# Adaptive attention and GRU on one core: score products in 64x32 tiles over two PSUM banks, V copied once and laid out by DMA, VectorE's order changed

## What is computed

```python
def _L0(x, emb, ...):                    # attention, 16 heads of 16
    scale, shift = jnp.split(emb @ W_emb + b_emb, 2, axis=-1)
    xn = _rms_norm(x, g_norm) * (1.0 + scale) + shift
    q, k, v = ...(xn @ W_qkv)
    q = _rms_norm(q, g_q); k = _rms_norm(k, g_k)
    attn = softmax(einsum('bhqd,bhkd->bhqk', q, k) * d ** (-0.5))
    o = einsum('bhqk,bhkd->bhqd', attn, v)
    return o + o @ W_out
x = x + _L0(x, cond[:, None, :], ...)
x = x + GRU(initial_state=cond, inputs=x, ...)   # 32 steps, one after another
```

## Time and profile before

| | |
|---|---|
| time, median of 3 runs | 385.61 us (385.48 to 385.67) |
| span of the profiled execution | 383.5 us |
| busy: PE, DVE, ACT, POOL | 92%, 68%, 70%, 55% |
| attention stage | to about 214 us |
| mean granted TensorE clock | 0.985 |
| chain that ended last | PE 81%, issue 5%, POOL 4%, ACT 4% |

### The profile page before, as it was taken

How to read it: one execution, slowest core, us unless ns; L and a number is a source line. 1 busy time by engine, 2 the same in 40 slices (tenths; PEclk the granted TensorE clock), 3 DMA queues, 4 the chain that set the end, 5 groups by cost and what they waited for, 6 DMA issues and landing times.

```text
span 383.5 us, 11231 instructions
## 1 busy us (share of the span) xinstructions
PE 354.0 (92%) x3795; PEld 305.9 (80%) x3795; DVE 260.9 (68%) x693; ACT 268.9 (70%) x760; POOL 210.3 (55%) x383
## 2 busy tenths in 40 slices
PE   4287999999999999999997899999999999999983
PEld 3165678778777877877775899999999999999982
DVE  3455888888898888889888355555555555555553
ACT  2468999999999999999873555555555555555552
POOL 5347777776777777677742244444444444434432
PEclk9679999999999999999999999999999999999999
DMA  8942211211221121122121000000000000000000
GB/s 264 361 156 57 58 43 43 57 44 43 53 55 38 44 55 43 40 55 50 45 55 24 1 2 29 27 29 27 27 27 27 27 27 27 27 27 27 28 30 27
DMA packets 14269, 20.39 MB, mean 53 GB/s; under 512 B 2578, under 2 KB 7076, under 8 KB 14244
## 3 DMA queue, kind: packets, MB, share of 16 engines
q1 hardware_dynamic: 13700, 18.76, 17.3%
q10 hardware_dynamic: 544, 1.31, 0.9%
HBM read 7.48 MB, written 4.19 MB: 30 GB/s over the span
## 4 chain that ended last, share of the span: by engine, by line
PE 81%; issue 5%; POOL 4%; ACT 4%; DVE 2%; DMA 2%; POOLq 0%; SPq 0%; DVEq 0%; ACTq 0%
PE bank L914 39%; PE bank L961 21%; PE bank L1095 7%; PE bank L1054 4%; PE bank L1108 4%; PE bank L1123 2%; DMA x_in<-in_x_dram 2%; PE bank L1004 2%; PE bank L1019 2%; POOL oT_lo L425 1%; POOL operands L401 1%; POOL xn L415 1%; PE bank L974 1%; ACT square_x L516 1%; ACT v_diag L600 0%
## 5 line engine op out<-in xcount | busy, mean ns | idle before, releaser
L961 PE MATMUL bank<-h,w_hh_sb 128*128 128x128 f32 x768 | 96.9, 275 | 1.4 <-DVE h L902 1.4
L961 PEld LDWEIGHTS bank<-h,w_hh_sb 128*128 128x128 f32 x768 | 91.1, 192 | 2.0 <-DVE h L902 1.8
L676 ACT ACTIVATE operands<-bank,bsum 128x128 f32<-128x128 f32 x64 | 23.6, 368 | 55.6 <-PE bank L961 52.7
L887 DVE SCALAR_TENSOR_TENSOR operands<-bank,vec_cols,operands 128x128 f32<-128x128 f32 x64 | 22.3, 349 | 52.5 <-ACT operands L676 52.5
L486 POOL TENSOR_TENSOR operands<-operands,h 128x128 f32<-128x128 f32 x64 | 29.5, 461 | 51.3 <-ACT operands L677 51.3
L914 PE MATMUL bank<-pair_hi,wih_hi 128*128 128x256 f32 x180 | 52.6, 292 | 0.0
L914 PE MATMUL bank<-pair_hi,wih_lo 128*128 128x256 f32 x180 | 50.2, 279 | 0.0
L914 PE MATMUL bank<-wqkv_hi,xn_hi 128*128 128x512 f32 (+1 forms) x128 | 47.5, 371 | 2.9 <-POOL xn_lo L435 2.9
L914 PE MATMUL bank<-pair_lo,wih_hi 128*128 128x256 f32 x180 | 50.2, 279 | 0.0
L600 ACT COPY v_diag<-bank 32x256 f32<-32x256 f32 x128 | 46.6, 364 | 2.2 <-PE bank L914 0.7
L493 POOL TENSOR_TENSOR operands<-h,x2T 128x256 f32<-128x256 f32 x32 | 23.2, 726 | 41.1 <-issue 30.3
(11 more groups left out here) (107 smaller groups left out, 868.5 us busy)
## 6 DMA issues: line engine op xcount, KB each, us to landing
operands<-operands SPq DMA_DIRECT2D x128, 64.0 KB, 2.0
x_in<-in_x_dram SPq DMA_DIRECT2D x8, 512.0 KB, 8.7
out_dram<-operands SPq DMA_DIRECT2D x16, 256.0 KB, 2.0
stage_w<-in_L_cond_W_qkv_dram ACTq DMA_DIRECT2D x1, 768.0 KB, 7.3
w_hh_sb<-in_L_cond_W_hh_dram SPq DMA_DIRECT2D x1, 768.0 KB, 9.5
stage_w<-in_L_cond_W_ih_dram SPq DMA_DIRECT2D x1, 768.0 KB, 7.4
w_emb_sb<-in_L_cond_W_emb_dram ACTq DMA_DIRECT2D x1, 512.0 KB, 4.6
stage_wo<-in_L_cond_W_out_dram SPq DMA_DIRECT2D x1, 256.0 KB, 6.1
```

Source lines behind the costliest of these rows:

```text
L676: act.activation(r_g[:, c, :], r_in, ACT.Sigmoid, bias=bsum[:, c:c + 1]).then_inc(r_ready[c], 1)
L887: dve.scalar_tensor_tensor(out=rh[:, c, :], in0=xnh[:, HN_COL:HN_COL + B], scalar=bhh[:, 2 * KC + c:2 * KC + c + 1], in1=r_g[:, c, :], op0 ...
L961: last = pe.matmul(dst, gate(w_hh_sb, name, c)[k], moving, start=k == 0 and (name == "n" or opens and name == "z"), stop=k == KC - 1, skip ...
```

## The change

- Scores: each score product is cut in two halves of 64 rows, in 64x32 tiles; half i writes to its own PSUM bank (p_s is now two banks). 32 matmuls of 128 columns replace 16 of 256, and k_diag shrinks to two blocks. The order of the heads in the score columns changes, and the PV products index it accordingly.
- PSUM: to free a bank, p_xT and p_w (output projection) share one. Hence new waits on PE: the transposes of xhat wait for x2_ready, the output projection for xmod_ready.
- V: one ACT copy of 128x256 into v_rows replaces four copies of 32x256; SP then issues four more DMAs per body that lay v_rows out in v_diag. The PV products wait for these.
- PE's order: transposes of q and k now come ahead of the scores, which stand right before the PV products.
- DVE's order: residual, qkn, recip, o_sb, Tp, oT, xmod, ss, ms4, maxima, logits. Exp now works in place on logits. ACT's and POOL's lists keep their order.

```diff
+        s_tiles = [p_s[:, BANK * i:BANK * i + D] for i in range(2)]
...
-        gru_banks = ((p_qkT, p_xT, p_qk[0], p_qk[1]), (p_vx2, p_s, p_o, p_w))
+        gru_banks = ((p_qkT, p_qk[0], p_qk[1], p_s[:, 0:BANK]), (p_vx2, p_s[:, BANK:2 * BANK], p_o, p_xTw))
...
+                v = group(base, u, LAG_V)
+                if v is not None:
+                    slot = (u - LAG_V) % 2
+                    if isinstance(v, int) and v == 0:
+                        sp.wait_ge(ones_ready, 2)
+                    sp.wait_ge(v_ready, v + 1)
+                    for b in range(GB):
+                        rows = slice(T * b, T * b + T)
+                        sp.dma_start(v_diag[rows, (u - LAG_V) % 4, b, :, :].rearrange("p h f -> p (h f)"),
+                                     v_rows[rows, slot, :, :].rearrange("p h f -> p (h f)"))\
+                          .then_inc(v_diag_ready[slot], 16)
...
-                    values(range(0, 2))
+                    act.copy(v_rows[:, (u - LAG_V) % 2, :, 0:DH],
+                             p_v.rearrange("p (h d) -> p h d", h=HEADS)).then_inc(v_ready, 1)
...
-                if v is not None:
-                    values(range(2, GB)).then_inc(v_ready, 1)
...
             def body(base, u):
+
+                if not draining(base, u):
+                    residual(group(base, u, LAG_OUT + 1), (u - LAG_OUT - 1) % 2)
+                g = group(base, u, LAG_QKT)
+                if g is not None:
+                    slot = (u - LAG_QKT) % 2
+                    dve.wait_ge(rs_ready, g + LAG_QK + 1)
+                    if later(g, 2):
+                        dve.wait_ge(qkT_ps, g - 1)
+                    dve.tensor_tensor(qkn[:, slot, :].rearrange("p (h d) -> p h d", d=DH),
...
                 o = group(base, u, LAG_OUT)
...
-                if not draining(base, u):
-                    residual(group(base, u, LAG_OUT + 1), (u - LAG_OUT - 1) % 2)
...
-                g = group(base, u, LAG_QKT)
-                if g is not None:
-                    slot = (u - LAG_QKT) % 2
-                    dve.wait_ge(rs_ready, g + LAG_QK + 1)
...
+                    d = group(base, u, LAG_X2T)
+                    if d is not None:
+                        pe.wait_ge(x2_ready, d + 1)
                     for c in range(KC):
                         last = pe.transpose(p_xT[:, c * P:c * P + P], xhat[:, (u - LAG_MOD) % 2, c * P:c * P + P],
...
+                    m = group(base, u, LAG_MOD)
+                    if m is not None:
+                        pe.wait_ge(xmod_ready, m + 1)
...
-                    pe.wait_ge(v_ready, g + 1)
+                    pe.wait_ge(v_diag_ready[(u - LAG_PV) % 2], spread(g, (u - LAG_PV) % 2))
...
+                if scores is not None:
+                    slot = (u - LAG_S) % 2
+                    for c in range(KC):
+                        for b in range(GB):
+                            for i in range(2):
+                                rows = slice(2 * PB * i, 2 * PB * i + 2 * PB)
+                                last = pe.matmul(s_tiles[i][T * b:T * b + T, c * P:c * P + P]
+                                                 .rearrange("p (r n k) -> p n r k", r=2, k=T),
+                                                 qkT[rows, slot, c * P + T * b:c * P + T * b + T],
+                                                 k_diag[rows, slot, :, :, GB * c + b, :], start=True, stop=True)
+                    last.then_inc(s_ps, 1)
```

More of the change, by code:

```diff
@@ L212, in adaptive_attention_gru @@
         v_ready = sem("v_ready")
+        v_diag_ready = [sem("v_diag_ready0"), sem("v_diag_ready1")]
         qkT_ps = sem("qkT_ps")
@@ L453, in _ @@
             pool.memset(threes[:, :], 3.0).then_inc(threes_ready, 1)
[L454 to L458, removed]
+            pool.memset(v_rows[:, :, :, DH:VW], 1.0).then_inc(ones_ready, 1)
+            pool.memset(v_diag[:, :, :, :, :], 0.0).then_inc(ones_ready, 1)
             pool.wait_ge(threes_ready, 1)
-            pool.wait_ge(ones_ready, 1)
+            pool.wait_ge(ones_ready, 2)
             first = [norm_first[:, i, :] for i in range(7)]
@@ L564, in body @@
                     act.wait_ge(logits_ready, g + 1)
-                    if later(g, 2):
-                        act.wait_ge(probsT_ready, g - 1)
-                    act.activation(probs[:, slot, :], logits[:, slot, :], ACT.Exp).then_inc(probs_ready, 1)
+                    act.activation(logits[:, slot, :], logits[:, slot, :], ACT.Exp).then_inc(probs_ready, 1)
                 if draining(base, u) and draining(base, u - 1):
@@ L595, in body @@
                        .then_inc(oT_hi_ready, 1)
[L597 to L602, removed]
                 v = group(base, u, LAG_V)
@@ L608, in body @@
                         act.wait_ge(o_ps, v - 3)
-                    if isinstance(v, int) and v == 0:
-                        act.wait_ge(ones_ready, 1)
+                    if later(v, 2):
+                        act.wait_ge(v_diag_ready[(u - LAG_V) % 2], spread(v - 2, (u - LAG_V) % 2))
                 d = group(base, u, LAG_X2T)
@@ L1032, in output_projection @@
                         pe.wait_ge(x2_ready, g)
-                    products(p_w[:, 0:D], [oT_hi[:, slot, c * P:c * P + P] for c in range(KC)],
+                    products(p_w, [oT_hi[:, slot, c * P:c * P + P] for c in range(KC)],
                              [oT_lo[:, slot, c * P:c * P + P] for c in range(KC)],
```

68 lines of the change are left out of this document (31 added, 37 removed).

## The result

The kernel after takes 401.25 us (median of 4 runs, 400.5 to 402.31), the kernel before 385.64 (4 runs, 385.48 to 385.79): a ratio of 1.0388, 95% interval 1.0358 to 1.0417. The forecast was 398.2 with a range of 391 to 403, and slower with 0.87. The profiled execution has a span of 398.6 us against 383.5.

A forecast was written before the change was run, and what follows sets the result against it. PE bounds the kernel at 5.61 us a body; the new DVE order closes a 6.09 us ring. Loop +12.0, filling +1.1, draining -0.5 give +12.6 on 383.5: 396.1, plus 2.1 for the median: 398.2 us, range 391 to 403.

The forecast's parts named there:

- rival 3: Attention loop: dependent instruction pairs cost more in the hardware loop; 6.3 us a body, 403 us; chance 0.13.
- The ring: Loop body: qkn through xmod, xn and Newton to the next qkn sets the pitch, 6.09 us against 5.61.
- the filling: Bodies 4 to 8: xmod 0.6 us later in body 4 and another 0.6 in body 8; +1.1 us, estimated.
- signs of being wrong: Attention loop: PE without holes near 5.1, qkn not released by rs, 1 us score block, PE waiting for a DMA.
- PE's block: Scores on PE: 1.00 us shrinks by 0.46 for the rounds, with 0.09 for one tile switch saved; about 0.55 long.
- Rival 5: Scores on PE: the row halves don't run side by side; PE's body 5.5 us, time unmoved; chance 0.1, inside the forecast.
- Rival 4: Score matmuls on PE: a fixed issue time binds; PE's body about 6.5 us, time about 408; chance 0.02.
- Rival 2: Loop body: only the ring through the residual counts; 5.57 to 5.65 us a body, 385 to 387 us; chance 0.05.
- the draining: From xmod of body 33 on: -1.35, about -0.3 and +1.1 us, together -0.5 us.
- the DMAs at SP: SP's list: eight DMAs take 4.8 us to issue, below any pitch considered, covered by several us; no cost.
- GRU stage: Stage after attention, with other banks and the same products: 0 us change.
- Rival 1: Attention loop: PE's saving comes through; pitch 5.1 us, -12.8 us, 373 us; chance 0.08.

The follow-up runs named there:

- late_v: Kernel after, with the last group's four V DMAs issued behind the last keys' DMAs at SP; 398.49 us, ratio 1.0326 to the kernel before.
- order_only: Kernel before with DVE's new order (residual and qkn at the top of the body) and nothing else; 404.7 us, ratio 1.0456.
- old_orders: Kernel after with DVE's and PE's old orders, except that the scores' waits stand ahead of the V products; 384.21 us, ratio 0.9936.
- half_v_late: half_v with ACT's v_rows copy first, its two direct copies behind exp, and the last V DMAs behind the last keys'; 379.22 us, ratio 0.9801.
- v_copies: old_orders, but V by ACT's four copies as before and no V DMAs; 385.29 us, ratio 0.9972 to the kernel before.
- old_dve_order: Kernel after with DVE's old order and PE's new order kept; 393.15 us, ratio 1.0167 to the kernel before.
- half_v: old_orders, but two of four sequences' V copied by ACT straight into v_diag, two by v_rows and DMA; 386.27 us, ratio 1.0006.

## Why the prediction was right, point by point

The measured time lies in the range. At 401.25 it is just above the 394 to 401 that the forecast gave to its own mechanism and inside the stretch that it gave to rival 3. The ring and its pitch came as forecast. Every other term came out on the slow side, and the missing 3 us are not rival 3's: they are the filling, the last group's DMAs, and how far the median lies above the profiled execution. One of the listed signs of being wrong did appear, at the ends of the stage alone: PE waited for a DMA before scores, 0.2 us once in the filling, then 0.24 and 2.29 for the last two groups.

**PE's block.** The score block was forecast at 0.55 and takes 0.59. The stretch in which the switches lie, from the last V product to the PV products, takes 150.96 - 149.72 = 1.24, against 147.57 - 145.78 = 1.79: 0.55 less, which is the forecast (0.46 for the rounds, 0.09 for a switch). The waits added on PE for the residual and for xmod appear in no view: between 60 and 200 us PE's only wait is that for oT_lo, 21.5 us in 23 bodies. Rival 5, halves not side by side, is out: eight rounds of 0.115 would take 0.92. The Trainium skill (TensorEngine Tiling (Array Packing), Key Properties) says that different tiles can load weights and multiply in parallel; the 0.59 agrees. Rival 4, issue, is out as well: 32 score matmuls in 0.59 are 0.018 each. By the 62 ns per MATMUL that the Trainium skill (TensorE: Matmul & The Clock Gate, Back-to-back issue gap) gives for hardware decoding off, they would take an estimated 2.0 us; this trace doesn't agree with that case. (The clock's digit in the earlier trace rows is 9 from the fourth slice on, not from the sixth; nothing in the prediction hangs on it.)

**The ring.** Step by step, forecast and measured:

| step | forecast | in the body from 150.64 |
|---|---|---|
| xmod, to its end | 0.38 | 0.39 |
| end of xmod to xn | 0.18 | 0.17 |
| xn to the first Newton step | 2.06 | 2.06 |
| Newton, to the end of the last | 1.24 | 1.24 |
| to qkn | 0.03 | 0.03 |
| qkn to recip | 0.60 | 0.61 |
| recip to o_sb | 0.29 | 0.28 |
| o_sb to Tp | 0.35 | 0.34 |
| Tp to oT | 0.63 | 0.63 |
| oT to xmod | 0.33 | 0.32 |
| sum | 6.09 | 6.07 |

Over 25 bodies that is 152.43 - 140.28 = +12.15 against +12.0. That the mean of 6.10 meets the forecast's 6.09 so closely is in part luck. The written-out bodies 8 to 10 take 5.98, the twenty of the hardware loop 6.12. From the end of xmod to xn is 0.08 in the former (52.92 + 0.38 to 53.39) and 0.18 in the latter, and the forecast took 0.18 for all. From the last Newton step to qkn is 0.12 instead of 0.03 in two of four loop bodies; in this one POOL's last step ends at 166.41 + 0.26 = 166.67:
```profile
166.79 0.69 DVE L772 TENSOR_TENSOR qkn<-bank,rs 128x512 f32<-128x512 f32 x1 [0.44 <-POOL rs L466]
```
In every fourth body xn comes 0.28 after xmod, but then Newton follows 1.95 after xn instead of 2.06, so this adds nothing. So rival 3's mechanism exists: the loop costs 0.14 a body over the written-out bodies, of which the forecast had 0.10 in its sum; the rest, and what the written-out bodies save, nearly cancel. The 1.95 is POOL's own work between the two, forecast at 1.93. PE's idle time before the output projection was forecast at 1.0 and is 0.91.

**Rival 2, the residual's ring.** The residual starts at 153.68 and would let qkn start 0.35 later, at 154.03; qkn starts at 154.53, released by rs. So that ring alone would give 6.07 - 0.50 = 5.57, which is the forecast's sum for it, and it is out as the limit.

**The filling: +1.1 forecast, +2.24 measured, but not all of it is the change's.** The xmods of bodies 2, 4, 5, 6, 7 and 8 are later than before by 0.34, 1.58, 2.34, 1.77, 1.62 and 2.24. In late_v, whose instructions are the same up to the draining, bodies 4 to 8 are later by 1.52, 1.80, 0.96, 0.79 and 1.41. The two part in body 5, where xmod waits 0.40 for PE in the kernel after (31.13) and not in late_v. Busy time of the same two us in the kernel after and in late_v (PE, PEld, DVE, ACT, POOL; then the granted clock, 1.00 being 2.4 GHz):
```profile
30.00:32.00 2.00, 2.00 (x10) 1.76 (x8) 1.56 (x3) 0.60 (x1) 1.37 (x3) 0.50 0.00 0
```
```profile
30.00:32.00 2.00, 1.39 (x11) 1.01 (x10) 1.78 (x4) 1.02 (x3) 1.56 (x2) 1.00 0.00 0
```
The granted clock was at its lower level (1.2 GHz) in this execution of the kernel after, and had been 0.73 in the two us before; late_v had 1.00 in both. Before the clock fell, PE had been busy for 2.47 of the 4 us from 22 on and for 0.53 of the next 2; in late_v for 3.44 and 0.47. No run tests what set the two apart. So 0.83 of the 2.24 belongs to the execution. Of the 1.41 that late_v has, 0.27 is loading: over the twelve kernels profiled here the first xmod starts anywhere from 14.50 to 15.05, and at 14.85 in order_only, which changes nothing ahead of it. The jump in body 8, 0.62, is recip and o_sb, as forecast with 0.6.

What remains is body 4, and here the +1.1 had luck. It counted 0.6 for the duration of qkn alone. Timeline of DVE there, in the kernel after:
```profile
25.12 0.69 DVE L772 TENSOR_TENSOR qkn<-bank,rs 128x512 f32<-128x512 f32 x1 [1.86 <-POOL rs L466]
25.73 0.41 DVE L820 TENSOR_TENSOR xmod<-bank,mod_scale 128x256 f32<-128x256 f32 x1
```
In body 4 xmod could start at 24.15 in the kernel before, when rs of that body was not there yet (24.51 + 0.26). Put behind qkn, xmod pays for qkn's wait as well as for its duration: 1.58 - 0.34 = 1.24. In an in-order list a moved instruction brings its wait along. That step was sized at half, but the bodies behind it make up for the other half, which the forecast had not in its sum either: in late_v 0.79 - 0.27 = 0.52 of it is left in body 7.

**The draining.** xmod of body 33 to qkn of body 34 is 203.06 - 199.36 = 3.70 instead of 5.25, so -1.55 for the -1.35 forecast; up to recip of body 36 it is -0.40, for the -0.5 forecast in all. Then comes what the prediction had set to nothing: the DMAs at SP. For the body it was right (SP has 4.9 of 6.1 us to do). It failed for the last group, where the keys' DMAs are what PE waits for and stand behind 2.50 us of V issues: +1.15, and late_v takes 1.39 off, more than all of it. Behind that wait the granted clock falls for some 4 us, which is in the +1.15 too. Busy time in stretches of the kernel after, columns as above:
```profile
217.00:219.70 2.70, 0.45 (x5) 0.26 (x3) 2.33 (x5) 0.83 (x3) 0.95 (x1) 1.00 0.32 74
219.70:222.00 2.30, 2.26 (x67) 1.69 (x67) 1.26 (x2) 0.00 (x0) 0.29 (x1) 0.58 0.00 0
222.00:224.00 2.00, 1.97 (x33) 1.71 (x35) 1.89 (x6) 1.00 (x3) 0.00 (x0) 0.63 0.01 4
```
PE was nearly idle from 217.0 to 219.7; then the clock is at its lower level (1.2 GHz) for most of two stretches (1.00 again from 224 on), and the score block, 0.59 in the loop, lasts 220.57 - 219.74 = 0.83. In the kernel before, where the last scores wait 0.48, and in late_v, where they wait 0.92, the granted clock is 1.00 in these stretches.

**The rest.** GRU stage: 0 forecast; from recip of body 39 to the end it is 174.3 before and 174.2 after. The median lies 2.65 above the span of the profiled execution, where 2.1 was taken from the kernel before; the profiled one was the shortest of the four runs. In sum: +12.0, +1.1, -0.5, 0 and 2.1 gave 398.2; +12.15, +2.24, +0.75, 0 and 2.65 give 401.3.

**What PE's and ACT's savings were worth.** The forecast said: hidden. old_orders shows them laid open in its late bodies (5.23), half_v_late shows them paid out (379.2). Rival 1 put them at 373, with a pitch of 5.1; what it missed is that the next limits, ACT with xn_hi and SP's issue, lie close: the pitches found here run from 5.2 to 5.6. Four of my expectations (old_orders, v_copies, old_dve_order, half_v) missed by 3 to 8 us: each took one limit away, and named the wrong next one, none, or one too small; old_orders and old_dve_order missed at the end of the stage besides.

## What to carry to other kernels

When an instruction moves ahead in an in-order list, look up who makes its input and on what that depends: if the way leads back to something now behind it in the same list, a ring through one loop body has closed, and its sum, not any engine's busy time, is the pitch. If the same work is dear inside the suspected ring and free outside it, the ring is real. The slack of the input (here 1.9 us between rs and qkn) is the first number to read; here the ring showed in the trace as engines that all waited, each for another, in every body. Before moving a wait, look at what now stands behind it. Count the issue time of DMAs as work of the engine that issues them, against the pitch hoped for and not the present one, and look at the last group apart, where no later body covers a late transfer.

## What the hardware showed

- Issuing a DMA from one part of SBUF to another costs SP 0.60 to 0.62 us here, with 64 KB (keys) and with 34 KB (V) alike: four in 2.41 to 2.50.
- In old_orders and the kernel after, up to about 90 us and again near the end of the stage, one of four such issues often takes 0.6 to 1.3 us longer (3.16, 3.62 and 3.25 us above). What else the chip does at that time I didn't find; the cause stays open.
- In the filling, one 128x33 step on POOL takes 0.66 us instead of 0.26, in both kernels, while DVE makes wo_lo from two tiles in SBUF. In the kernel after, newton_b (L462) starts at 28.67 and lasts 0.66, DVE's wo_lo (L746) starts at 28.53 and lasts 0.69: POOL's step ends 0.11 after DVE's. The Trainium skill (SBUF — State Buffer, SBUF: two separate sides) says that a VectorE instruction with two SBUF inputs and a GpSimd one that reads SBUF lock each other out; these rows agree.
